# Filling the empty edge slots of a two-layer graph kernel with spread row numbers

## Chip, cores and metric

One NeuronCore of one Trainium2 chip. The metric is the device time of one execution in microseconds (us); a lower number is better. Three runs of the kernel before are at hand, and one further execution was recorded by the hardware profiler.

## What is computed

A graph of 6250 nodes (128 features, f32) and 206,250 directed edges (`src`, `dst`) goes through two attention layers.

```python
h = jnp.maximum(_layernorm(x), 0.0)
x = x + layer0(h)      # per edge: q of src, k and v of dst, 8 heads, clip, exp, sum over edges of src, normalise
h = jnp.maximum(_layernorm(x), 0.0)
x = x + layer1(h)      # per edge: cosine of h[src] and h[dst] times beta, softmax over edges of src, sum of h[dst]
```

In both layers every edge needs one row of a table in HBM by its `dst`, and the result is summed by its `src`.

## The kernel before, in words

**Sorting.** `sort_and_project` sorts the edges by the block of 128 nodes that `src` lies in (49 blocks). The edges stand as 128 partitions x 1620 columns and are taken in 18 chunks of 90 columns (NCHUNK, CHUNK). Edges of one chunk and block are laid into rows of 4 slots (ROW). One slot is an int32, `dst * 256 + (src & 127) + 1` (PACK is 256), and a slot with a low byte of 0 matches no node. Rows are written to the DRAM tensor `sorted_edges` by indirect DMAs of POOL (L389, 23 per chunk, 414 in all). A block's rows are padded to whole groups of 128 rows. A group is thus 128 partitions x 4 slots = 512 slots (GT is 4), and the arrays hold GROUPS = 456 groups, NT = 1824 slots per partition. Counted from the edge list, 439 groups hold edges; the last 17, groups 439 to 455, hold none. In the last group of each of the 49 blocks a part of the upper partitions is empty too: 4309 rows in all, some 88 of the 128 as a mean. The third kind of empty slot, inside rows that the sort does write (1282 slots), comes from the sort's own matmul and is 0.

**The fill.** Since only rows with edges are written, the slots of `sorted_edges` must hold something before the sort begins. DVE sets the SBUF tile `slots` to 0 (L596; it is part of the tile `slot_words`), SP waits for it and stores it to `sorted_edges` (L291, L292), then POOL waits until that store has landed (`s_filled`) and overwrites `slot_words` with `row_no`, an iota of 2944 elements (L381). ACT reads `row_no` at L532. On SP's queue the loads of the weights, gamma, beta and `cos_beta` stand behind the store (L294 to L297), and the stores of the counts (L301) behind those. POOL's queue holds the constants (L349 to L378) ahead of L381 and the 414 scatters after it. At the end of the sort, SP loads `slots` back (L342). DVE then splits them in place: the low byte less 1 goes to `loc`, and the upper bits, the row number to gather, stay in `slots`.

**The edge layers.** `layer0_edges` and `layer1_edges` walk over all 456 groups. For every group POOL issues four indirect DMAs, one for each slot column (L830 in `gather_groups`), each of which fetches 128 rows, one per partition: of `kv_table`, 1024 bytes a row, in layer 0, and of `h_table`, 520 bytes a row, in layer 1. The destinations are rings of 8 groups (`kv_rows`) and 12 groups (`h_rows`); before a group POOL waits for its row numbers (ACT, L934 and L1216) and for the ring slot's last reader: DVE's `vx` (L1013) in layer 0, PE's sums (L1294) in layer 1. DVE waits for the gathers of a group at L1005 (layer 0) and L1336 (layer 1), the first operations that read the gathered rows. PE multiplies by one-hot matrices made from `loc` (L968 and L982 in layer 0; L1264, L1277, L1286, L1294 in layer 1), and DVE adds up in SBUF (L1036, L1319). The last group of layer 0 must be added up before `between_layers` starts (L1099), and that of layer 1 before `finish` (L1380). An empty slot is gathered like any other; its one-hot row is zero, so what was fetched adds nothing.

Of the kernel before, what the change touches and what calls it, by code (L numbers as in the profile page):

```python
# [15 lines left out]
P = 128  # L16
N = 6250
# [34 lines left out]
ROOM = GROUPS + NCHUNK * CG  # L52
NT = GT * GROUPS
PACK = 256

RING0 = 8
NEAR = 4
# [47 lines left out]
def sort_and_project(nc, mem, dram, ins):  # L105

    src, dst, x, wq, wk, wv, gamma, beta, cos_beta = ins
    with ExitStack() as ctx:
# [3 lines left out]
        def sem(name):  # L112
            return ctx.enter_context(nc.semaphore(name))
# [3 lines left out]
        slots, loc_f, blkid, gb_sb, cb_sb = mem["slots"], mem["loc"], mem["blkid"], mem["gb"], mem["cb"]  # L117
# [77 lines left out]
        s_pool = sem("s_pool")  # L195
        s_pads = sem("s_pads")
        s_src, s_dst, s_x, s_w, s_gb = (sem(n) for n in ("s_src", "s_dst", "s_x", "s_w", "s_gb"))
        s_filled = sem("s_filled")
        s_v = sem("s_v")
        s_prep = sem("s_prep")  # L200
# [55 lines left out]
        def every_chunk(eng, chunk):  # L256

            turns = NCHUNK // 2
            for r in range(2 * PEEL):
                chunk(r // 2, r % 2)  # L260
            with eng.Fori(PEEL, turns - 1) as t:
                for r in range(2):
                    chunk(t, r)
            for r in range(2):
                chunk(turns - 1, r)
# [6 lines left out]
        def tiles_of(t, r, half):  # L272

            if isinstance(t, int) and not 1 <= t < NCHUNK // 2 - 1:
                return None
            s = 2 * r + half
            return 4 * t - 4 + s, (t - 1) * (4 * QT - 1) + QT * s, QT - s // 3

        def load_ends(eng, tile, edges, done):

            for a, b in ((0, 96), (96, 112), (112, P - 1)):
                if a == 96:
                    eng.wait_ge(s_pads, 2)
                eng.dma_start(tile[a:b, :], edges[a * COLS:b * COLS].rearrange("(p c) -> p c", c=COLS)).then_inc(done, 16)
            eng.dma_start(tile[P - 1:P, 0:LASTROW],
                          edges[(P - 1) * COLS:E].rearrange("(p c) -> p c", p=1)).then_inc(done, 16)

        @block.sync
        def _(sp):
            load_ends(sp, src_i, src, s_src)  # L290
            sp.wait_ge(s_pads, 4)  # L291
            sp.dma_start(slots_d, slots[:, :]).then_inc(s_filled, 16)  # L292
            for k, w in enumerate((wq, wk, wv)):
                sp.dma_start(w_sb[:, k * D:(k + 1) * D], w).then_inc(s_w, 16)  # L294
            for k, w in enumerate((gamma, beta)):
                sp.dma_start(gb_sb[:, k, :], w.rearrange("(o f) -> o f", o=1).broadcast_to((P, D))).then_inc(s_gb, 16)
            sp.dma_start(cb_sb[:, 0:1], cos_beta.rearrange("(o f) -> o f", o=1).broadcast_to((P, 1))).then_inc(s_gb, 16)  # L297

            for g in range(NCHUNK // CSTORE):
                sp.wait_ge(s_cntrow, CSTORE * (g + 1))  # L300
                sp.dma_start(dram["counts"][g * CSTORE:(g + 1) * CSTORE, :].rearrange("(o k) n -> o k n", o=1),  # L301
                             cnt_row[:, g % 2, :, :]).then_inc(s_cntd[g % 2], 16)
            for r in range(2):
                sp.wait_ge(s_cntd[r], 16 * (NCHUNK // CSTORE // 2))
            sp.dma_start(cnt[:, :].rearrange("b (k j) -> b k j", j=STEP),
                         dram["counts"].rearrange("k (b j) -> b k j", j=STEP)).then_inc(s_cntb, 16)

            sp.wait_ge(s_offc, 1)
            for part in range(2):
                sp.dma_start(dram["offs"][part].rearrange("k (b j) -> b k j", j=STEP),  # L310
                             off_parts[:, part, :].rearrange("b (k j) -> b k j", j=STEP)).then_inc(s_offd, 16)
            sp.wait_ge(s_offd, 32)
            for r in range(2):
                sp.dma_start(offrow[:, r:r + 1, :], dram["offs"][:, r:r + 1, :]).then_inc(s_row[r], 16)

            def stores(t, r):

                for half in range(2):
                    tiles = tiles_of(t, r, half)  # L320
                    if tiles:
                        s, first_tile, n = tiles
                        sp.wait_ge(s_hnow, s + 1)
                        sp.dma_start(h_sb[:, ds(first_tile, n), :], h_now[:, half, 0:n, :]).then_inc(s_hd[half], 16)
                for half in range(2):
                    tiles = tiles_of(t, r, half)
                    if tiles:
                        s, first_tile, n = tiles
                        sp.wait_ge(s_kv, s + 1)
                        sp.dma_start(dram["kv"].rearrange("(t p) f -> p t f", p=P)[:, ds(first_tile, n), :],  # L330
                                     kv[:, half, 0:n, :]).then_inc(s_kvd[half], 16)

            def loads(t, r):
                if not (isinstance(t, int) and t == NCHUNK // 2 - 1):
                    sp.wait_ge(s_rank, SPC * (2 * t + r) + 1)
                    sp.dma_start(offrow[:, r:r + 1, :], dram["offs"][:, ds(2 * t + r + 2, 1), :]).then_inc(s_row[r], 16)
                stores(t, r)
            every_chunk(sp, loads)
            sp.wait_ge(s_sorted, 1)
            sp.dma_start(slots[:, :], slots_d).then_inc(s_back, 16)  # L340
            for half in range(2):
                sp.wait_ge(s_kvd[half], 16 * (NCHUNK - 4))  # L342
                sp.wait_ge(s_hd[half], 16 * (NCHUNK - 4))
            sp.wait_ge(s_gb, 48)
            sp.wait_ge(s_filled, 16)

        @block.gpsimd
        def _(pool):
# [16 lines left out]
                                    base=0, pattern=[[1, P]], channel_multiplier=-1).then_inc(s_const, 1)  # L365
            nc.gpsimd.affine_select(out=ident[:, :], in_=ident[:, :], compare_op=ALU.not_equal, fill=1.0,
                                    base=0, pattern=[[-1, P]], channel_multiplier=1).then_inc(s_const, 1)
            nc.gpsimd.affine_select(out=keep[:, :], in_=keep[:, :], compare_op=ALU.not_equal, fill=0.0,
                                    base=-NBLK, pattern=[[0, 1]], channel_multiplier=1).then_inc(s_const, 1)
            nc.gpsimd.affine_select(out=room[:, :], in_=room[:, :], compare_op=ALU.is_equal, fill=0.0,  # L370
                                    base=-NBLK, pattern=[[0, NCHUNK]], channel_multiplier=1).then_inc(s_const, 1)
            nc.gpsimd.affine_select(out=bidiag[:, :], in_=bidiag[:, :], compare_op=ALU.not_equal, fill=1.0,
                                    base=0, pattern=[[-1, P]], channel_multiplier=1).then_inc(s_pool, 1)
            pool.wait_ge(s_pool, 6)
            nc.gpsimd.affine_select(out=bidiag[:, :], in_=bidiag[:, :], compare_op=ALU.not_equal, fill=-1.0,
                                    base=1, pattern=[[-1, P]], channel_multiplier=1).then_inc(s_pool, 1)
            pool.wait_ge(s_pool, 7)
            nc.gpsimd.affine_select(out=bidiag[:, :], in_=bidiag[:, :], compare_op=ALU.not_equal, fill=1.0,  # L378
                                    base=-NBLK, pattern=[[N, P]], channel_multiplier=1).then_inc(s_const, 1)
            pool.wait_ge(s_filled, 16)  # L380
            nc.gpsimd.iota(row_no, [[1, CG * P]], base=0, channel_multiplier=0,  # L381
                           allow_small_or_imprecise_dtypes=True).then_inc(s_const, 1)
# [209 lines left out]
        def _(dve):  # L592
            nc.vector.memset(src_i[96:P, LASTROW:COLS], PAD_SRC).then_inc(s_pads, 1)
            nc.vector.memset(dst_i[96:P, LASTROW:COLS], 0).then_inc(s_pads, 1)
            nc.vector.memset(x_sb[:, LASTB, :], 0.0).then_inc(s_pads, 1)
            nc.vector.memset(slots[:, :], 0).then_inc(s_pads, 1)  # L596
            nc.vector.memset(ones_b[:, :], 1.0).then_inc(s_prep, 1)
            nc.vector.memset(ones_2[:, :], 1.0).then_inc(s_prep, 1)
            tt, ts, stt = nc.vector.tensor_tensor, nc.vector.tensor_scalar, nc.vector.scalar_tensor_tensor
# [26 lines left out]
            link(ts(src_i[:, :], src_i[:, :], P - 1, None, ALU.bitwise_and))  # L626
            link(ts(pk_f[:, :], dst_i[:, :], float(PACK), 1.0, ALU.mult, ALU.add))
            tt(pk_f[:, :], pk_f[:, :], src_i[:, :], ALU.add).then_inc(s_packed, 1)
# [149 lines left out]
            for m in range(SPC):  # L778
# [10 lines left out]
            dve.wait_ge(s_back, 16)  # L789
            link(nc.vector.tensor_scalar(loc_f[:, :].bitcast(i32), slots[:, :], PACK - 1, None, ALU.bitwise_and))  # L790
            link(nc.vector.tensor_scalar(loc_f[:, :], loc_f[:, :].bitcast(i32), -1.0, None, ALU.add))
            link(nc.vector.tensor_scalar(slots[:, :], slots[:, :], PACK.bit_length() - 1, None,
                                         ALU.logical_shift_right))
# [656 lines left out]
```

## Time and profile before

| | us |
|---|---|
| median of 3 runs | 5818.73 |
| lowest and highest | 5814.07 and 5819.33 |
| the profiled execution | 5821.99 |
| its span, first to last instruction | 5820.3 |

| engine | busy us | share of the span |
|---|---|---|
| PE matmul | 4527.6 | 78% |
| POOL | 4147.2 | 71% |
| DVE | 4060.3 | 70% |
| ACT | 2159.7 | 37% |

The profiled execution's own time lies 1.7 us above its span and 3.3 us above the median of the runs. In the trace, the sort lasts until about 891, layer 0 gathers from 892 to 3250 and ends at 3288, layer 1 gathers from 3433 to 5754 and ends at 5797; the output is stored until 5820. "Busy" leaves out the issue of plain DMAs; POOL's indirect DMAs are counted as busy for the time in which POOL builds their descriptors, not for the transfer. Granted clock 1.00 in a stretch is TensorE's 2.4 GHz level, and 0.50 is 1.2 GHz.

### The profile page before, as it was taken

What the parts mean: (1) busy time and instruction counts of PE and PEld (TensorE: products, weight loads), DVE (VectorE), ACT (ScalarE), POOL (GpSimd) and SP (SyncE); (2) the same over time, 40 slices, a digit from 0 to 9 for tenths busy, and PEclk for the clock granted to TensorE, in tenths of its full rate; (3) what the DMA queues carried; (4) which work ended last, traced back from release to release, by engine and by line L of the source; (5) the groups of instructions that cost most, each with busy time, mean ns of one, the idle gap of its engine ahead of it and who ended that gap; (6) DMA issues with size and microseconds to landing.
All of it is one profiled execution on the core that took longest, in us unless ns stands there. A gap on an engine that the chain in (4) does not pass through costs nothing. (4 is left out here: it accounts for less than half of the span.)

```text
span 5820.3 us, 108286 instructions
## 1 busy us (share of the span) xinstructions
PE 4527.6 (78%) x25285; PEld 3846.5 (66%) x25286; DVE 4060.3 (70%) x11508; ACT 2159.7 (37%) x8114; POOL 4147.2 (71%) x4084
## 2 busy tenths in 40 slices
PE   5888866777777777777777338989888888888887
PEld 2777755666656666666655227878787778777776
DVE  8988956666766666666666676666666666666665
ACT  4988850000000000000000025555556555555554
POOL 0788877777777777777777237777777777777773
PEclk7888866666676666666666557777878888888886
DMA  1000003333333333333334422222222222222227
GB/s 43 15 18 18 18 5 98 101 101 101 101 102 102 102 102 102 102 102 102 101 102 96 42 44 55 54 53 54 54 51 54 54 54 53 54 53 54 53 53 50
DMA packets 192388, 388.47 MB, mean 67 GB/s; under 512 B 78472, under 2 KB 102546, under 8 KB 192150
## 3 DMA queue, kind: packets, MB, share of 16 engines
q0 software_dynamic: 159168, 361.59, 27.1%
q1 hardware_dynamic: 31146, 20.67, 1.4%
q10 hardware_dynamic: 1836, 4.03, 0.3%
q14 instruction: 209, 1.71, 0.1%
q8 instruction: 29, 0.48, 0.0%
HBM read 367.60 MB, written 15.20 MB: 66 GB/s over the span
## 5 line engine op out<-in xcount | busy, mean ns | idle before, releaser
L830 POOL DMA_INDIRECT h_rows<-h_table,idx_ring x1824 | 1745.4, 957 | 758.6 <-issue 533.7
L830 POOL DMA_INDIRECT kv_rows<-kv_table,idx_ring x1824 | 1803.6, 989 | 556.5 <-issue 555.3
L968 PE MATMUL psum<-q_sb,hotT 128*128 x3648 | 784.9, 383 | 435.5 <-DVE prod L1005 434.2
L968 PEld LDWEIGHTS psum<-q_sb,hotT 128*128 128x128 f32 x3648 | 678.7, 278 | 543.9 <-issue 543.4
L982 PE MATMUL psum<-vx,hot 128*128 128x136 f32 x3648 | 837.9, 399 | 151.6 <-DVE acc L1036 150.1
L947 ACT ACTIVATE vx<-clip 128x32 f32<-128x32 f32 x456 | 104.5, 229 | 2242.7 <-DVE clip L1029 2242.7
L982 PEld LDWEIGHTS psum<-vx,hot 128*128 128x128 f32 x3648 | 722.5, 286 | 317.5 <-issue 245.1
L389 POOL DMA_INDIRECT sorted_edges<-stage,addr x414 | 587.5, 1419 | 275.5 <-ACT stage L539 149.6
L1005 DVE TENSOR_TENSOR prod<-psum,kv_rows 128x512 f32<-128x512 f32 x456 | 315.3, 691 | 630.8 <-DMA kv_rows<-kv_table,idx_ring 630.1
L1336 DVE SCALAR_TENSOR_TENSOR prod<-psum,h_rows 128x128 f32<-128x128 f32 x1824 | 529.3, 346 | 240.3 <-DMA h_rows<-h_table,idx_ring 227.8
L1294 PE MATMUL psum<-h_rows,hotw 128*128 128x129 f32 x3648 | 652.0, 333 | 0.0
L1264 PE MATMUL psum<-q_sb,acc 128*128 x3648 | 620.3, 326 | 21.4 <-DVE prod L1336 20.7
L1264 PEld LDWEIGHTS psum<-q_sb,acc 128*128 128x128 f32 x3648 | 579.0, 241 | 29.8 <-issue 28.7
L1224 ACT ACTIVATE hotl<-hot,logit 128x128 f32<-128x128 bf16 x1824 | 589.5, 394 | 0.0
L1224 ACT ACTIVATE hotw<-hot,wgt 128x128 f32<-128x128 bf16 x1824 | 587.3, 393 | 0.2
L562 ACT ACTIVATE ends<-is_place,pk_now 128x92 f32<-128x92 bf16 x1440 | 517.3, 451 | 134.7 <-DVE is_place L748 134.5
L1294 PEld LDWEIGHTS psum<-h_rows,hotw 128*128 128x128 f32 x3648 | 565.6, 236 | 0.0
L1319 DVE SCALAR_TENSOR_TENSOR h_sb<-h_sb,corr,psum 128x129 f32 x456 | 159.1, 349 | 574.8 <-issue 379.8
L1277 PE MATMUL psum<-ident,hotl 128*128 128x128 f32 x1824 | 347.2, 321 | 268.4 <-DVE gmax L1329 267.4
L855 PE MATMUL psum<-rows,pick_row 4*128 4x512 bf16 x912 | 431.4, 473 | 154.6 <-DMA rows<-loc_rows 154.1
L1286 PEld LDWEIGHTS psum<-newtop,acc 128*128 128x128 f32 x3648 | 538.1, 226 | 0.3 <-issue 0.3
L1286 PE MATMUL psum<-newtop,acc 128*128 128x1 f32 x3648 | 517.4, 263 | 0.1
(206 smaller groups left out, 5994.5 us busy)
## 6 DMA issues: line engine op xcount, KB each, us to landing
kv_rows<-kv_table,idx_ring POOLq DMA_INDIRECT x1824
h_rows<-h_table,idx_ring POOLq DMA_INDIRECT x1824
sorted_edges<-stage,addr POOLq DMA_INDIRECT x414, 2.3
kv_table<-kv SPq DMA_DIRECT2D x21, 256.0 KB, 2.1
rows<-loc_rows SPq DMA_DIRECT2D x228, 4.0 KB
h_table<-acc SPq DMA_DIRECT2D x1, 3185.0 KB, 19.2
out<-q_sb SPq DMA_DIRECT2D x2, 1536.0 KB
h_sb<-h_now SPq DMA_DIRECT2D x21, 128.0 KB, 2.0
```

The source lines that it names most:

```text
L389: pool.indirect_dma_start(out=dram["sorted"], out_offset=bass.IndirectOffsetOnAxis(ap=addr[:, r, g:g + 1], axis=0), in_=stage[:, r, g * RO ...
L562: last = nc.scalar.activation(to_place[:, k, c, :], is_place[:, k, :, c], ACT.Copy, scale=pk_now[:, r, BATCH * b + c:BATCH * b + c + 1])
L830: pool.indirect_dma_start(out=G[:, u, j, :], out_offset=None, in_=table, in_offset=bass.IndirectOffsetOnAxis(ap=idx[:, u, j:j + 1], axis=0 ...
L855: nc.tensor.matmul(out, pick_row[:, g_u % FOUR, :], rows[:, h, :], start=True, stop=True).then_inc(s_spread, 1)
L968: last = nc.tensor.matmul(Q_ps[k][:, j * P:(j + 1) * P], hotT[:, k, j * P:(j + 1) * P], q_sb[:, ds(blk, 1), :].rearrange("p o f -> p (o f) ...
L982: last = nc.tensor.matmul(S_ps[(u - 3) % 2], hot[:, k, j * P:(j + 1) * P], vx[:, k, j, :], start=(j == 0), stop=(j == GT - 1))
L1224: last = nc.scalar.activation(out[:, j * P:(j + 1) * P], hot[:, u, :, j], ACT.Copy, scale=scale[:, j:j + 1])
L1264: last = nc.tensor.matmul(Q_ps[k][:, j * P:(j + 1) * P], hotT[:, (u + 1) % RING1, j * P:(j + 1) * P], q_sb[:, ds(blk, 1), :].rearrange("p ...
L1277: last = nc.tensor.transpose(L_ps[u % 2][:, j * P:(j + 1) * P], hotl[:, (u - 2) % TRIO, j * P:(j + 1) * P], ident[:, :])
L1286: last = nc.tensor.matmul(E_ps[u % 2][:, j:j + 1], hotT[:, n, j * P:(j + 1) * P], newtop[:, n:n + 1], start=True, stop=True)
L1294: last = nc.tensor.matmul(S_ps[u % 2], hotw[:, (u - 8) % TRIO, j * P:(j + 1) * P], G[:, (u - 8) % RING1, j, 0:AW1], start=(j == 0), stop=( ...
L1336: last = nc.vector.scalar_tensor_tensor(prod[:, j * P:(j + 1) * P], Q_ps[u % 2][:, j * P:(j + 1) * P], G[:, u, j, D + 1:TW], G[:, u, j, 0: ...
```

## The change

The zero fill by DVE goes. POOL writes the tile instead, by an iota after its constants: slot column j of partition p gets the value `256 * j + p * 34 * 256`. Its low byte is 0, so it matches no node, and its upper bits name row `j + 34 * p`. FILL_STEP is (6250 - 1824) // 127 = 34, and the highest row is 1823 + 34 * 127 = 6141. In one gather of 128 partitions the empty slots then name rows that stand 34 apart, 34,816 bytes in `kv_table` and 17,680 bytes in `h_table`. SP waits for POOL's `s_filler` in place of DVE's fourth `s_pads`.

```diff
+FILL_STEP = (N - NT) // (P - 1)
...
+        s_filler = sem("s_filler")
...
         def _(sp):
             load_ends(sp, src_i, src, s_src)
-            sp.wait_ge(s_pads, 4)
+            sp.wait_ge(s_filler, 1)
             sp.dma_start(slots_d, slots[:, :]).then_inc(s_filled, 16)
...
                                     base=-NBLK, pattern=[[N, P]], channel_multiplier=1).then_inc(s_const, 1)
+            nc.gpsimd.iota(slots[:, :], [[PACK, NT]], base=0, channel_multiplier=FILL_STEP * PACK).then_inc(s_filler, 1)
             pool.wait_ge(s_filled, 16)
...
             nc.vector.memset(x_sb[:, LASTB, :], 0.0).then_inc(s_pads, 1)
-            nc.vector.memset(slots[:, :], 0).then_inc(s_pads, 1)
```

## Rows read from the trace of the kernel before

**Rows 1.** The page: DMA share in 40 slices of the span, in tenths.
```profile
DMA  1000003333333333333334422222222222222227
```
**Rows 2.** The page, costliest groups: busy, mean ns of one, idle before, releaser.
```profile
L830 POOL DMA_INDIRECT h_rows<-h_table,idx_ring x1824 | 1745.4, 957 | 758.6 <-issue 533.7
L830 POOL DMA_INDIRECT kv_rows<-kv_table,idx_ring x1824 | 1803.6, 989 | 556.5 <-issue 555.3
```
**Rows 3.** Waits of POOL inside layer 0, 900 to 3160: total us, times, longest.
```profile
POOL kv_rows L830 <- issue: 532.4, 1747, 0.3
```
**Rows 4.** Windows: stretch, PE, PEld, DVE, ACT, POOL busy, clock, DMA share, GB/s.
```profile
2400.00:2900.00 500.00, 384.36 (x1642) 308.50 (x1643) 347.29 (x678) 30.38 (x194) 382.36 (x387) 0.66 0.36 102
...
3179.00:3250.00 71.00, 45.79 (x181) 36.30 (x182) 39.61 (x77) 3.19 (x19) 54.24 (x56) 0.60 0.90 78
4400.00:4900.00 500.00, 436.33 (x2878) 392.45 (x2878) 333.74 (x1580) 294.09 (x1188) 379.46 (x396) 0.83 0.24 54
5670.00:5760.00 90.00, 81.06 (x386) 72.80 (x387) 47.04 (x222) 40.70 (x159) 56.75 (x60) 0.59 0.95 41
```
**Rows 5.** Timeline of POOL, layer 0: start, us; fourth gathers of groups 438 and 455.
```profile
3161.84 0.95 POOL L830 DMA_INDIRECT kv_rows<-kv_table,idx_ring  x1 [0.30 <-issue]
...
3249.80 0.95 POOL L830 DMA_INDIRECT kv_rows<-kv_table,idx_ring  x1 [0.30 <-issue]
```
**Rows 6.** Timeline of DVE, layer 0: first use of groups 438, 439, 455; next stage.
```profile
3164.61 0.69 DVE L1005 TENSOR_TENSOR prod<-psum,kv_rows 128x512 f32<-128x512 f32 x1 [1.41 <-DMA kv_rows<-kv_table,idx_ring]
...
3172.14 0.69 DVE L1005 TENSOR_TENSOR prod<-psum,kv_rows 128x512 f32<-128x512 f32 x1 [3.75 <-DMA kv_rows<-kv_table,idx_ring]
...
3279.04 0.69 DVE L1005 TENSOR_TENSOR prod<-psum,kv_rows 128x512 f32<-128x512 f32 x1 [3.41 <-DMA kv_rows<-kv_table,idx_ring]
...
3287.80 0.56 DVE L1099 TENSOR_SCALAR rden<-acc 128x392 f32<-128x392 f32 x1 [0.33 <-PEq L860]
```
**Rows 7.** Timeline of POOL, layer 1: fourth gathers of groups 438, 447, 455.
```profile
5659.02 0.95 POOL L830 DMA_INDIRECT h_rows<-h_table,idx_ring  x1 [0.30 <-issue]
...
5704.08 0.95 POOL L830 DMA_INDIRECT h_rows<-h_table,idx_ring  x1 [0.30 <-issue]
...
5753.84 0.94 POOL L830 DMA_INDIRECT h_rows<-h_table,idx_ring  x1 [0.30 <-issue]
```
**Rows 8.** Timeline of DVE, layer 1: first use of groups 438, 455; next stage.
```profile
5661.62 0.35 DVE L1336 SCALAR_TENSOR_TENSOR prod<-psum,h_rows 128x128 f32<-128x128 f32 x1 [0.71 <-DMA h_rows<-h_table,idx_ring]
...
5774.84 0.35 DVE L1336 SCALAR_TENSOR_TENSOR prod<-psum,h_rows 128x128 f32<-128x128 f32 x1 [1.42 <-DMA h_rows<-h_table,idx_ring]
...
5797.29 0.47 DVE L1380 RECIPROCAL den<-h_sb 128x49 f32<-128x49 f32 x1 [0.33 <-PEq L1139]
```
**Rows 9.** Waits of POOL in layer 1, 3430 to 5797.
```profile
POOL h_rows L830 <- ACT idx_ring L1216: 184.9, 11, 181.9
```
**Rows 10.** Windows of 10 us in layer 1, columns as in rows 4.
```profile
4320.00:4330.00 10.00, 10.00 (x45) 9.34 (x46) 4.04 (x18) 5.37 (x21) 5.67 (x6) 0.50 0.20 47
...
5690.00:5700.00 10.00, 10.00 (x45) 9.33 (x45) 5.67 (x26) 5.93 (x24) 7.59 (x8) 0.50 0.93 41
```
**Rows 11.** Timeline of POOL at the start.
```profile
6.46 0.51 POOL L359 IOTA start<- 128x456 f32 x1
...
8.70 0.29 POOL L378 TENSOR_SCALAR_AFFINE_SELECT bidiag<-bidiag 128x128 f32<-128x128 f32 x1
14.72 2.58 POOL L381 IOTA slot_words<- 128x2944 f32 x1 [5.72 <-DMA sorted_edges<-slot_words]
```
**Rows 12.** Timeline of SP's queue at the start.
```profile
5.47 0.36 SPq L292 DMA_DIRECT2D sorted_edges<-slot_words  x1
...
26.71 48.26 SPq L301 DMA_DIRECT2D column_counts<-to_part  x6
```
**Rows 13.** Timeline of DVE at the start.
```profile
12.28 1.00 DVE L604 TENSOR_SCALAR pk_f<-ends 128x1620 int32<-128x1620 int32 x1 [6.70 <-DMA ends<-in_src]
```
**Rows 14.** Timeline of ACT: first read of `row_no`.
```profile
85.87 2.73 ACT L532 ACTIVATE start<-slot_words,edge 50x2944 bf16<-50x2944 f32 x1
```

## The prediction

> **What bounds the kernel now.** I read the page first, then the waits, then windows of 10 to 500 us, and last the timelines at the two ends of the edge layers.
>
> The row of DMA shares shows the sort, then layer 0 (tenths of 3), then layer 1 (tenths of 2). The last slice of each layer stands out: a 4 and a 7 [rows 1]. The costliest groups are POOL's gathers, 1824 in each layer. In layer 0 POOL is busy 1803.6 us and idle 556.5, together 2360.1 or 5.18 us for each of 456 groups [rows 2]. Its idle time consists of gaps of at most 0.3 us that nothing releases [rows 3], so in layer 0 POOL issues without pause and never waits for its ring. The layer cannot end before POOL's last issue, and as long as gathers land quickly it ends just behind it. In layer 1 POOL is busy 1745.4 and idle 758.6 [rows 2], 181.9 of it in one wait before the first group [rows 9]. Of the remaining 576.7, layer 0's plain gaps make 556.5, so 20.2 us are true stalls. Unstalled, a group costs (1745.4 + 556.5) / 456 = 5.05 us. Layer 1 is bound by POOL's issue as well, for nearly all of its length.
>
> The windows show what happens to the transfers [rows 4]. In mid-layer the 16 DMA engines are busy 0.36 of the time and move 102 GB/s (layer 0), 0.24 and 54 GB/s (layer 1). In the two tails, where only empty groups are left, they are busy 0.90 and 0.95 of the time and move only 78 and 41 GB/s. Full engines would move 102 / 0.36 = 283 and 54 / 0.24 = 225 GB/s of ordinary rows, but 87 and 43 GB/s in the tails: the same gather of the same size is 3.3 and 5.2 times as slow. The one thing special in these groups is that all 512 slots name row 0.
>
> The end of layer 0 says what that costs. Group 438, the last with edges, is used 3164.61 - 3161.84 = 2.77 us after its fourth gather was issued. Group 455 is used 3279.04 - 3249.80 = 29.24 us after its own [rows 5, 6]. Between groups 439 and 455 the uses stand (3279.04 - 3172.14) / 16 = 6.68 us apart, while POOL issues a group each (3249.80 - 3161.84) / 17 = 5.17 us. The transfers fall behind and DVE waits for them before each use.
>
> **The change, part by part.**
>
> *Layer 0, tail.* The empty groups now name 128 different rows per gather. If those move like ordinary rows, the use follows the issue by 2.77 us again: 29.24 - 2.77 = **26.5 us saved**. POOL's own pace stays as it is, since it was not stalled. The 8.8 us from the last use to the next stage (3287.80 - 3279.04 [rows 6]) stay. How much slower than ordinary rows may the new ones be? POOL offers 4 x 128 x 1024 bytes in 5.17 us, 101 GB/s, against 283: they may be 2.8 times as slow before anything shows. I take full saving; the bounds are 0 (as slow as row 0) and 26.5.
>
> Here a rule can be held against the row. The Trainium skill (DMA: Bandwidth & Descriptors, section Anatomy of one DMA) fits one DMA issued by POOL as 2.0 us plus its bytes over 436 GB/s, so 2.3 us for these 131,072 bytes and 2.15 us for a gather of layer 1. By that fit the two tails together would give back some 1.3 us more than by the rows; I keep the rows.
>
> *Layer 1, tail.* It has two terms. The delay from fourth gather to first use is 5661.62 - 5659.02 = 2.60 us for group 438 and 5774.84 - 5753.84 = 21.00 us for group 455 [rows 7, 8]. PE sometimes lags a little in this layer, so I take 3.0 for the ordinary delay: 18.0 us. And here POOL did stall: late gathers held back PE's sums, whose end frees a ring slot. The 8 groups from 447 to 455 took 5753.84 - 5704.08 = 49.8 us [rows 7]; at 5.05 each they take 40.4. That is 9.4 us more, and together **27.4 us saved**. The 22.4 us from the last first use to `finish` [rows 8] stay. The margin is larger than in layer 0: 266,240 bytes in 5.05 us are 53 GB/s against 225. Bounds: 0 and 27.8 (with the delay of 2.60).
>
> *Partly empty groups.* The last group of each block has some 88 rows of row 0 per gather. In layer 0 POOL never waits [rows 3], so nothing is won there. In layer 1, 20.2 - 9.4 = 10.8 us of stalls lie before the tail. Windows show that stretches of low TensorE clock can make such stalls: at a granted clock of 0.50 PE is busy 10.00 of 10 us and POOL gets through 6 gathers where it usually has 8, with a DMA share of only 0.20, so no slow gather [rows 10]. I take 0 here; bounds 0 and 10.8 saved.
>
> *The front.* DVE's fill goes; DVE then waits 6.70 us for `in_src` anyway [rows 13], worth nothing. POOL's iota over 1824 elements isn't in the trace. Between 456 elements in 0.51 us and 2944 in 2.58 us [rows 11] the slope is 0.83 ns an element, which gives 1.65 us; bounds 0.51 and 2.58. It starts at 8.70 + 0.29 = 8.99, ends near 10.7, and SP's store goes out 5.2 us later than at 5.47 [rows 12]. Behind it on SP's queue, the loads of weights, gamma, beta and `cos_beta` slip as much; the next entry, the first store of counts, is only due at 26.71 [rows 12], 16 us later, and six issues lie between (the store's own took 0.36 us). On POOL, L381 waits for the store. The store of 912 KB was issued at 5.47 and let L381 go at 14.72 [rows 11], 9.2 us; from 10.7 that gives 19.9, and the iota of `row_no` ends near 22.5. Its reader starts at 85.87 [rows 14]. So 63 us cover it. Without that cover the store's delay would cost 5.2 us, which is the upper bound; the lower is 0.5 us gained, should `in_src` land earlier. I take 0.
>
> *Sum.* 26.5 + 27.4 = 53.9 us. Against the profiled execution's own 5821.99 this gives 5768.1. The median of the runs is 3.3 lower, so the forecast is 5764.8, rounded to **5765 us**. By its bounds and the spread of the runs shown (5.3 us) this case covers 5757 to 5773.
>
> **The rivals.**
>
> *More is won.* The 10.8 us of stalls inside layer 1 could stem from the partly empty groups, one in nine, whose slow gathers let PE wait and its clock fall. Then the time is near 5754. Against it: 49 such groups and only half a tail's worth of stalls, and the low-clock window of rows 10 has no slow gather in it. Chance 0.10.
>
> *Layer 1 gives nothing back, since PE is the bound there.* In the old tail PE is busy 10.00 of 10 us at a clock of 0.50 with 45 matmuls [rows 10], just as in the mid-layer window where POOL made 6 gathers in 10 us, or 6.7 us a group. If PE stays low through the whole tail, 17 groups take 113 us from 5661.62, which ends at 5775: no gain over 5774.84. Only layer 0's 26.5 remain, 5792. Against it: over 4400 to 4900 the mean clock is 0.83, over the tail 0.59 [rows 4], so the fall goes with the late gathers. A low stretch of 50 us near the end would cost 7.5 groups x 1.6 = 12 us, 5777. Chance 0.06 for a loss beyond that.
>
> *Nothing changes, since row 0 isn't the cause.* If an empty group were slow whatever it names, the time stays at 5819. The ordinary rows of the same queue, size and destination speak against this. 
>
> *Slower.* The new rows stand 34 apart in every gather. If such a regular step falls on fewer parts of HBM than one row does, the tails get longer. The point is 6.68 us a group: beyond it by 0.34 us (5%), the 34 empty groups cost over 11.6 us. At twice the time of row 0 it would be 34 x 6.7 = 228 us, 6047. Nothing in the trace has this pattern; 128 different rows can hardly be worse than one. Chance 0.02.
>
> **How the numbers follow.** The forecast gets what is left, 0.79. The range of 5752 to 5780 holds it, the case with more won, and a low clock of 50 us near the end; some 0.1 lies outside. A difference of 0.2% (11.6 us) is about what a measurement of this kernel can tell from none. All cases but the last two are faster by more: 0.95 faster, 0.03 same, 0.02 slower.
>
> **What the changed profile would show.** DMA tenths of 3 and 2 up to each layer's end; in the tails DMA shares near 0.36 and 0.24; DVE's last L1005 some 3 us behind POOL's last gather, and L1336 likewise; POOL's idle time in layer 1 down by about 9 us. At the front, a POOL iota of 1.7 us and L381 near 20 us, with L532 still at 86. Wrong would be: full DMA engines in the tails (the rows collide), PE at 10.00 with clock 0.50 and POOL stalled at the end of layer 1 (PE binds), or a later L532.

## The result, and the profile after

The changed kernel takes 5811.49 us (median of 20 runs, 5798.51 to 5830.88), the kernel before 5824.65 us (20 runs, 5801.65 to 5844.35). The ratio is 0.998, with a 95% interval of 0.9971 to 0.9989. The change gains 13 us where 54 were forecast. The profiled execution has a span of 5798.8 us against 5820.3. Further down, one of the four executions of experiment e10 was a slow one, 6858.07 us at a granted clock of 1.00 where the three others show 0.74, and is left out of its numbers.

The page of the changed kernel, DMA shares in 40 slices, and the two groups of gathers (L832 is the old L830):

```profile
DMA  1000003333333333333333122222222222222222
...
L832 POOL DMA_INDIRECT h_rows<-h_table,idx_ring x1824 | 1767.6, 969 | 720.9 <-issue 523.8
L832 POOL DMA_INDIRECT kv_rows<-kv_table,idx_ring x1824 | 1818.4, 997 | 556.6 <-issue 555.0
```

Windows of the changed kernel, columns as in [rows 4]:

```profile
3179.00:3250.00 71.00, 55.31 (x232) 44.41 (x231) 47.46 (x95) 4.04 (x24) 54.39 (x55) 0.64 0.35 102
...
5670.00:5750.00 80.00, 70.19 (x450) 64.63 (x448) 52.37 (x251) 44.50 (x175) 61.38 (x62) 0.80 0.24 52
```

The busy DMA engines at the layers' ends are gone [rows 1, 4]. In the tails the shares are 0.35 and 0.24 at 102 and 52 GB/s, as in mid-layer. Timeline of the changed kernel, POOL's last gather and the first use of its group, layer 0 then layer 1 (5709.03 is the fourth gather of group 447):

```profile
3262.05 0.98 POOL L832 DMA_INDIRECT kv_rows<-kv_table,idx_ring  x1 [0.30 <-issue]
...
3264.88 0.69 DVE L1007 TENSOR_TENSOR prod<-psum,kv_rows 128x512 f32<-128x512 f32 x1 [2.20 <-DMA kv_rows<-kv_table,idx_ring]
3273.42 0.56 DVE L1101 TENSOR_SCALAR rden<-acc 128x392 f32<-128x392 f32 x1 [0.33 <-PEq L862]
...
5709.03 0.95 POOL L832 DMA_INDIRECT h_rows<-h_table,idx_ring  x1 [0.31 <-issue]
...
5750.59 0.95 POOL L832 DMA_INDIRECT h_rows<-h_table,idx_ring  x1 [0.30 <-issue]
...
5753.41 0.35 DVE L1338 SCALAR_TENSOR_TENSOR prod<-psum,h_rows 128x128 f32<-128x128 f32 x1 [1.00 <-DMA h_rows<-h_table,idx_ring]
```

The delay is 2.83 us in layer 0 (it was 29.24) and 2.82 us in layer 1 (21.00). So 26.4 and 18.2 us came back, where 26.5 and 18.0 were forecast. POOL's stalls at the end of layer 1 are gone too: the 8 groups from 447 to 455 take 5750.59 - 5709.03 = 41.6 us, and took 49.8 [rows 7]. What took most of it away again is in the middle: POOL's last gather of layer 0 is at 3262.05 instead of 3249.80 [rows 5], though the first one is 2.6 us earlier (889.0 instead of 891.6). All of POOL's gathers by their durations (minimum, median and maximum in ns), kernel before, then the changed one:

```profile
L830 POOL DMA_INDIRECT kv_rows<-kv_table,idx_ring x1824: 942/947/1445, 891.6 to 3249.8; - x183
L830 POOL DMA_INDIRECT h_rows<-h_table,idx_ring x1824: 939/945/1207, 3432.6 to 5753.8; - x183
```

```profile
L832 POOL DMA_INDIRECT kv_rows<-kv_table,idx_ring x1824: 949/954/1510, 889.0 to 3262.1; - x183
L832 POOL DMA_INDIRECT h_rows<-h_table,idx_ring x1824: 946/952/1217, 3416.8 to 5750.6; - x183
```

Minimum and median are both 7 ns higher, in both layers. POOL's busy time grows from 1803.6 to 1818.4 and from 1745.4 to 1767.6 us, 37.0 us in all. The account of the two spans: sort -2.6, first to last gather of layer 0 +14.8, delay -26.4, drain -0.2, from L1101 to layer 1's first gather -1.4, first to last gather of layer 1 +12.6, delay -18.2, the rest -0.1. That is -21.5, the whole difference. In layer 1, the 22.2 us of longer gathers are partly offset, because the stalls fall from 20.2 to 720.9 - 153.8 - 556.6 = 10.5 us; the 153.8 is POOL's wait for its first row numbers, the longest of the six in this line:

```profile
POOL h_rows L832 <- ACT idx_ring L1218: 155.3, 6, 153.8
```

The front of the changed kernel, POOL, SP's queue and DVE:

```profile
8.95 1.65 POOL L382 IOTA slot_words<- 128x1824 int32 x1
20.19 2.59 POOL L384 IOTA slot_words<- 128x2944 f32 x1 [9.59 <-DMA sorted_edges<-slot_words]
...
10.62 0.36 SPq L294 DMA_DIRECT2D sorted_edges<-slot_words  x1
...
13.30 1.00 DVE L606 TENSOR_SCALAR pk_f<-ends 128x1620 int32<-128x1620 int32 x1 [9.63 <-DMA ends<-in_src]
```

The iota took 1.65 us, SP's store left at 10.62, and `row_no` was ready near 22.8, long before its reader at 85.8. The front costs nothing, as forecast. (That layer 0 starts 2.6 us earlier isn't the change's doing: in e1, the kernel before once more, it starts at 889.3.) The front is also where the loss is set off, as the experiments show.

### The profile page after: what moved, and what is told of

The parts are those of the page before. It is cut to its first block and busy times, and to the rows that moved or that the text cites. A ratio compares the mean times of both kernels' runs of the same rounds, so it can differ in the third digit from the quotient of the medians.

```text
span 5798.8 us, 108286 instructions
## 1 busy us (share of the span) xinstructions
PE 4597.1 (79%) x25285; PEld 3902.6 (67%) x25286; DVE 4048.6 (70%) x11507; ACT 2159.4 (37%) x8114; POOL 4183.7 (72%) x4085
## 5 line engine op out<-in xcount | busy, mean ns | idle before, releaser
L832 POOL DMA_INDIRECT h_rows<-h_table,idx_ring x1824 | 1767.6, 969 | 720.9 <-issue 523.8
L832 POOL DMA_INDIRECT kv_rows<-kv_table,idx_ring x1824 | 1818.4, 997 | 556.6 <-issue 555.0
L970 PE MATMUL psum<-q_sb,hotT 128*128 x3648 | 801.4, 388 | 379.9 <-DVE prod L1007 379.2
L984 PE MATMUL psum<-vx,hot 128*128 128x136 f32 x3648 | 867.9, 410 | 139.9 <-DVE acc L1038 138.0
L984 PEld LDWEIGHTS psum<-vx,hot 128*128 128x128 f32 x3648 | 749.3, 295 | 307.2 <-issue 233.1
```

Source lines behind the costliest of these rows:

```text
L832: pool.indirect_dma_start(out=G[:, u, j, :], out_offset=None, in_=table, in_offset=bass.IndirectOffsetOnAxis(ap=idx[:, u, j:j + 1], axis=0 ...
L970: last = nc.tensor.matmul(Q_ps[k][:, j * P:(j + 1) * P], hotT[:, k, j * P:(j + 1) * P], q_sb[:, ds(blk, 1), :].rearrange("p o f -> p (o f) ...
L984: last = nc.tensor.matmul(S_ps[(u - 3) % 2], hot[:, k, j * P:(j + 1) * P], vx[:, k, j, :], start=(j == 0), stop=(j == GT - 1))
```

## The experiments

e1 to e4 ran on one chip, e5 to e8 on a second, e9 to e12 on a third, e13 to e16 on a fourth, e17 and e18 on a fifth, each time with the kernel before beside them. The ratio is to that one. "Gathers" is the median duration in layer 0, in ns, from the one profiled execution of each; the times are medians of 3 to 12 executions.

| run | POOL's added instruction | fill | gathers | median us | ratio (95% interval) |
|---|---|---|---|---|---|
| e1 | none | 0 | 946 | 5817.37 | 0.9998 (0.9987 to 1.0009) |
| e2 | int32 iota, full | spread | 954 | 5812.45 | 0.9984 (0.9975 to 0.9994) |
| e3 | int32 iota, full | 0 | 957 | 5853.97 | 1.0056 (1.0037 to 1.0076) |
| e4 | none | spread | 946 | 5773.90 | 0.9917 (0.9903 to 0.9930) |
| e5 | int32 memset, 1 element | spread | 949 | 6988.06 | 1.0006 (0.9996 to 1.0016) |
| e6 | int32 iota, 1 element | spread | 953 | 6984.31 | 0.9996 (0.9987 to 1.0006) |
| e7 | int32 iota, full; a memset less | spread | 957 | 6987.75 | 1.0000 (0.9990 to 1.0009) |
| e8 | int32 iota, full; 3 int32 memsets | spread | 957 | 6987.69 | 1.0003 (0.9993 to 1.0013) |
| e9 | as e2 | spread | 954 | 5805.82 | 0.9975 (0.9962 to 0.9988) |
| e10 | as e4 | spread | 946 | 5762.81 | 0.9899 (0.9874 to 0.9925) |
| e11 | as e3 | 0 | 954 | 5858.29 | 1.0066 (1.0046 to 1.0087) |
| e12 | as e2, as the first | spread | 954 | 5803.52 | 0.9975 (0.9963 to 0.9987) |
| e13 | f32 memset, 1 element | spread | 946 | 5770.16 | 0.9923 (0.9898 to 0.9948) |
| e14 | f32 iota, 1 element | spread | 949 | 5769.64 | 0.9917 (0.9896 to 0.9937) |
| e15 | int32 iota, 1 element | spread | 957 | 5808.49 | 0.9991 (0.9975 to 1.0008) |
| e16 | f32 iota, full, cast by DVE | spread | 946 | 5777.87 | 0.9934 (0.9910 to 0.9958) |
| e17 | int32 memset, 1 element | spread | 946 | 6971.37 | 0.9996 (0.9986 to 1.0005) |
| e18 | two int32 iotas, 1 element | spread | 953 | 6966.52 | 0.9987 (0.9978 to 0.9997) |

**Both kernels again, on one chip (e1, e2).** No edit.

> 

> The kernel before, once more, with a profile from the chip that the three others of this job run on. Theory T (row 0 is slow, the spread is not, and something else made POOL's gathers slower) and rival C (the slower issue is the chip's, not the change's) both expect ratio 1.000 and the two slow tails (last L1005 29 us behind the last gather). C expects POOL's gathers at the same median on this chip as in the changed kernel; T expects 0.947 us here and 0.953 us there.

> 

> The changed kernel, once more, on the same chip. T: POOL's gathers have a median of 0.953 us against 0.947 in the kernel before, together some 37 us more busy time over 3648 gathers, so the ratio is 0.997 to 0.998 though the tails give back 54 us. C (only another chip): POOL is as fast as in the kernel before on this chip, and the ratio is near 0.991.

The gathers of layer 0, e1 then e2:

```profile
L830 POOL DMA_INDIRECT kv_rows<-kv_table,idx_ring x1824: 942/946/1437, 889.3 to 3242.0; - x183
```

```profile
L832 POOL DMA_INDIRECT kv_rows<-kv_table,idx_ring x1824: 949/954/1413, 888.9 to 3262.6; - x183
```

On the same chip the 7 to 8 ns stay. The difference belongs to the kernel; the chip as its cause (C) is out.

**The iota without the spread (e3).**

```diff
-            nc.gpsimd.iota(slots[:, :], [[PACK, NT]], base=0, channel_multiplier=FILL_STEP * PACK).then_inc(s_filler, 1)
+            nc.gpsimd.iota(slots[:, :], [[0, NT]], base=0, channel_multiplier=0).then_inc(s_filler, 1)
```

> 

> The changed kernel with the iota's steps set to 0, so it writes zeros: POOL's added instruction and the new wait stay, the spread goes. Theory A (the added instruction in POOL's stream slows its later gathers): gathers at 0.953 us, tails slow as before, ratio 1.004 to 1.007. Theory B (the row numbers slow POOL's issue, by the traffic they make): gathers at 0.947 us and ratio 1.000. C: ratio 1.000.

```profile
L832 POOL DMA_INDIRECT kv_rows<-kv_table,idx_ring x1824: 952/957/1328, 889.1 to 3259.2; - x183
```

The gathers are slow though every empty slot names row 0, and the kernel is 33 us slower than before. In its tail the DMA engines are full again; window of e3, columns as in [rows 4]:

```profile
3180.00:3250.00 70.00, 43.61 (x171) 34.28 (x172) 37.07 (x72) 3.04 (x19) 53.56 (x55) 0.63 0.96 78
```

So the traffic of the spread rows does not slow the issue (B falls), and the slow tail comes from row 0.

**The spread without a POOL instruction (e4).** The zero fill stays. DVE adds the partition number to it (`rho`) and multiplies by 34 * 256, and SP waits for that.

```diff
-            sp.wait_ge(s_pads, 4)
+            sp.wait_ge(s_filler, 1)
...
+            dve.wait_ge(s_pads, 4)
+            dve.wait_ge(s_const, 4)
+            nc.vector.tensor_scalar(slots[:, :], slots[:, :], rho[:, 0:1], float(FILL_STEP * PACK), ALU.add,
+                                    ALU.mult).then_inc(s_filler, 1)
```

> 

> The kernel before, with POOL's instructions untouched; DVE adds the partition number times 34 * 256 to its zero fill (row 34p in every column). The 128 rows of a gather are all different. Theory A: gathers at 0.947 us, no slow tails, ratio 0.990 to 0.992 (54 us saved). Theory B: gathers at 0.953 us and ratio 0.997 to 0.998. If rows that repeat from gather to gather are slow too, the tails stay partly.

```profile
L836 POOL DMA_INDIRECT kv_rows<-kv_table,idx_ring x1824: 942/946/1356, 888.1 to 3245.7; - x183
L836 POOL DMA_INDIRECT h_rows<-h_table,idx_ring x1824: 938/944/1209, 3401.2 to 5716.9; - x183
```

Timeline of e4: the last gather of layer 0, its use, and the first use of the last group in layer 1:

```profile
3245.75 0.95 POOL L836 DMA_INDIRECT kv_rows<-kv_table,idx_ring  x1 [0.30 <-issue]
...
3248.51 0.69 DVE L1011 TENSOR_TENSOR prod<-psum,kv_rows 128x512 f32<-128x512 f32 x1 [2.14 <-DMA kv_rows<-kv_table,idx_ring]
...
5719.45 0.35 DVE L1342 SCALAR_TENSOR_TENSOR prod<-psum,h_rows 128x128 f32<-128x128 f32 x1 [0.74 <-DMA h_rows<-h_table,idx_ring]
```

Delays of 2.8 and 2.6 us and gathers of 946 ns together: 47 us faster than before, and 38.6 us faster than e2 beside it. POOL's busy time tells the same: 1803.4 + 1748.3 here, 1819.0 + 1767.0 in e2, 34.3 us. The 8 ns of median difference, over 3648 gathers, are 29 of these. It also shows that the same 128 rows may repeat from gather to gather without harm. Nothing between 128 different rows and one row for all was tried.

**Small instructions of two kinds, and a compensated count (e5 to e8).** e5 and e6 are e4 with one more POOL instruction where the changed kernel has its iota; e7 and e8 are edits of the changed kernel. `spare` is a new int32 tile of 8 columns that nothing reads.

```diff
e5: +            nc.gpsimd.memset(spare[:, 0:1], 0)
e6: +            nc.gpsimd.iota(spare[:, 0:1], [[0, 1]], base=0, channel_multiplier=1)
e7: -            nc.gpsimd.memset(keep[:, :], 1.0).then_inc(s_pool, 1)
e7: +            nc.vector.memset(keep[:, :], 1.0).then_inc(s_pool, 1)
e8: +            nc.gpsimd.memset(spare[:, 0:1], 0)      # and two more
```

> 

> The spread written by DVE (e4) plus one POOL memset of one element per partition where the changed kernel has its iota. Theory A1 (any instruction added ahead shifts POOL's later instructions, and their place in the stream sets the price): gathers at a median near 0.953 us instead of 0.946, ratio 0.996 to 0.999. Theory A2 (the int32 iota itself leaves POOL slower): gathers at 0.946 us, ratio 0.991 to 0.993.

> 

> The same with an int32 iota of one element per partition in place of the memset. A1: slow gathers (0.953 us) as in e5. A2: slow gathers here though not in e5. If neither is slow, it is the length of the iota, or the wait that hangs on it.

> 

> The changed kernel, and the memset of keep moved from POOL to DVE, so that POOL has as many instructions as before. A1: gathers back at 0.946 us, ratio 0.991 to 0.993 (54 us saved and none given back). A2: gathers stay at 0.953 us, ratio 0.997 to 0.999.

> 

> The changed kernel with three small POOL memsets more, so four instructions are added in all. A1 with a short period (four instructions of 64 bytes are one line of 256): gathers back at 0.946 us, ratio 0.991 to 0.993. A1 with another period: some other duration between 0.94 and 0.96. A2: 0.953 us.

The times of e5 to e8 tell nothing, since on this chip the kernel before itself took 6987.84 us. Waits of e5:

```profile
DVE hotT L1007 <- remote: 916.8, 114, 17.7
...
POOL kv_rows L838 <- DVE vx L1021: 643.5, 123, 12.5
```

POOL waits for DVE here, and layer 0 needs (3850.0 - 894.7) / 456 = 6.48 us a group, so neither 7 ns on a gather nor a transfer time of 6.68 us matters much. Why DVE stands still for up to 17.7 us was not tried. The durations of the gathers can still be read: 949 with the memset, 953 with the one-element iota, 957 in e7 and e8. Restoring POOL's count of instructions (e7) does not restore the gathers, and four instructions are no better than one (e8). So the place in the stream (A1) falls as the cause of the changed kernel's loss, and the kind is left. The levels are not quite those that A2 expected: 949 in e5 instead of 946, 957 in e7 instead of 953. The next runs had to say what a step of 3 ns means.

**Is the level the kernel's own? (e9 to e12).** Three repeats, and the changed kernel with its iota moved ahead of all of POOL's others.

```diff
+            nc.gpsimd.iota(slots[:, :], [[PACK, NT]], base=0, channel_multiplier=FILL_STEP * PACK).then_inc(s_filler, 1)
             nc.gpsimd.iota(bucket_no, [[1, NBUK], [0, CHUNK]], base=0, channel_multiplier=0,
...
-            nc.gpsimd.iota(slots[:, :], [[PACK, NT]], base=0, channel_multiplier=FILL_STEP * PACK).then_inc(s_filler, 1)
```

> 

> The changed kernel again, to see whether the level of POOL's gathers belongs to the kernel or to the load of a program. Theory K (it belongs to the kernel): the commonest duration is 0.953 us in layer 0 again. Theory R (it is drawn anew at each load): any of 0.946, 0.949, 0.953, 0.957. Where this chip binds the layers by POOL's issue, K expects ratio 0.997 to 0.999.

> 

> The spread written by DVE again. K: commonest gather 0.946 us and, where POOL binds, ratio 0.991 to 0.993. R: any level, and a ratio up to 1.001.

> 

> Zeros written by POOL's iota again. K: commonest gather 0.957 us, ratio near 1.0056 where POOL binds. R: any level.

> 

> The changed kernel with the iota as POOL's first instruction instead of after the constants; the later instructions stand in the same places of the stream as in the changed kernel, only those before move by one. If the place of the gather loops in the stream sets the level: 0.953 us as in the changed kernel. If what ran just before matters: another level. The store of the fill starts some 4 us earlier, which is hidden.

Neither K nor R is wholly right. The changed kernel is at 954 for the third time and e10 at 946 for the second, but the zero fill, at 957 in e3, is now at 954. Two later repeats show the same: e5 and e17 are one kernel at 949 and 946, e6 and e15 one kernel at 953 and 957. There are two families, 946 or 949 without an int32 iota and 953 or 957 with one (give or take 1); the step inside a family changes from run to run for the same kernel. Each repeat ran on another chip, so whether the step is drawn by the chip or at each start of the program stays open. Putting the iota first changes nothing (e12), so what ran just before the gathers does not matter either.

**The kind of instruction (e13 to e16).** e13 to e15 are e4 with one small POOL instruction each. e16 writes the changed kernel's fill as f32 and lets DVE turn it into int32; SP then waits for both.

```diff
e13: +            nc.gpsimd.memset(spare[:, 0:1], 0.0)
e14: +            nc.gpsimd.iota(spare[:, 0:1], [[0, 1]], base=0, channel_multiplier=1,
e14: +                           allow_small_or_imprecise_dtypes=True)
e15: +            nc.gpsimd.iota(spare[:, 0:1], [[0, 1]], base=0, channel_multiplier=1)
e16: +            nc.gpsimd.iota(slots[:, :].bitcast(f32), [[PACK, NT]], base=0, channel_multiplier=FILL_STEP * PACK,
e16: +                           allow_small_or_imprecise_dtypes=True).then_inc(s_filler, 1)
...
e16: +            dve.wait_ge(s_filler, 1)
e16: +            nc.vector.tensor_copy(slots[:, :], slots[:, :].bitcast(f32)).then_inc(s_filler, 1)
```

> 

> The spread by DVE (e4) plus one f32 memset of one element per partition on POOL, a kind that POOL's stream already has. Theory N (any added POOL instruction makes the later gathers slower): commonest gather in layer 0 above 0.946 us. Theory I (only an int32 iota does): 0.946 us. Where POOL binds, I expects ratio 0.990 to 0.992.

> 

> The same with an f32 iota of one element, again a kind that the stream already has. N: above 0.946 us. I: 0.946 us and ratio 0.990 to 0.992.

> 

> The same with an int32 iota of one element, as in e6, on another chip. I: 0.953 us, and where POOL binds a ratio of 0.996 to 0.999, since 3648 gathers at 7 ns and the longer ones that come with them cost 30 to 37 us. N: the same level as e13 and e14.

> 

> The changed kernel's fill, written by POOL as an f32 iota of the full size and turned into int32 by DVE, which is idle then. I: 0.946 us, no slow tails, ratio 0.990 to 0.992: the whole gain with the fill still on POOL. N: 0.949 to 0.957 us, ratio 0.995 to 1.000.

Gathers of layer 0 in e14, e15 and e16:

```profile
L839 POOL DMA_INDIRECT kv_rows<-kv_table,idx_ring x1824: 945/949/1421, 886.6 to 3246.9; - x183
```

```profile
L838 POOL DMA_INDIRECT kv_rows<-kv_table,idx_ring x1824: 952/957/1328, 892.8 to 3270.6; - x183
```

```profile
L835 POOL DMA_INDIRECT kv_rows<-kv_table,idx_ring x1824: 942/946/1277, 886.5 to 3243.6; - x183
```

`spare` is f32 in e14 and int32 in e15; otherwise they differ in nothing but the flag that the type needs. One int32 iota of one element costs 5808.49 - 5769.64 = 39 us. A full-size f32 iota costs nothing to be seen (e16). Theory I holds in all but the 949 of e14, where it expected 946: that is the step inside the family, and e14's time is that of e13. N falls, since e13 and e16 are at 946.

**Any int32 instruction, and twice (e17, e18).**

```diff
e17: +            nc.gpsimd.memset(spare[:, 0:1], 0)
e18: +            nc.gpsimd.iota(spare[:, 0:1], [[0, 1]], base=0, channel_multiplier=1)
e18: +            nc.gpsimd.iota(spare[:, 1:2], [[0, 1]], base=0, channel_multiplier=1)
```

> 

> The spread by DVE plus one int32 memset of one element on POOL, as in e5, on another chip. If only the int32 iota matters: commonest gather in layer 0 0.946 or 0.949 us and, where POOL binds, ratio 0.990 to 0.993. If any int32 instruction does: 0.953 or 0.957 us and 0.997 to 0.999.

> 

> The spread by DVE plus two int32 iotas of one element. If each such iota adds its 7 ns to all later gathers: 0.960 to 0.964 us, and a ratio near 1.004. If the first one changes a state once and for all: 0.953 or 0.957 us, ratio 0.997 to 1.000.

```profile
L838 POOL DMA_INDIRECT kv_rows<-kv_table,idx_ring x1824: 942/946/1404, 897.9 to 3841.2; - x183
```

```profile
L839 POOL DMA_INDIRECT kv_rows<-kv_table,idx_ring x1824: 949/953/1377, 894.9 to 3839.8; - x183
```

This chip too had the kernel before at 6975.98 us, so only the durations count. An int32 memset leaves the gathers at 946, and a second int32 iota adds nothing to the first. This fits a state that one int32 iota brings about and that lasts to the end of the program. The indirect DMAs of the sort, which stand behind the iota too, agree in their shortest one; kernel before, then the changed one:

```profile
L389 POOL DMA_INDIRECT sorted_edges<-stage,addr x414: 954/1144/3571, 166.9 to 879.3; - x138
```

```profile
L392 POOL DMA_INDIRECT sorted_edges<-stage,addr x414: 963/1143/3582, 166.5 to 876.8; - x138
```

But in every run here all indirect DMAs come after the iota. No run has it between two of them, so that it must be executed first, and not only be part of the program, is not shown.

## Why the prediction was wrong

- **What bounds the kernel: right.** POOL's issue bounds both layers. That is why 7 ns on an instruction of 0.95 us are seen in the total at all.
- **Tails: right.** Forecast delays of 2.77 and 3.0 us, measured 2.83 and 2.82, counted from the start of the issuing instruction, so 26.4 and 18.2 us came back. The Trainium skill's fit (DMA: Bandwidth & Descriptors, section Anatomy of one DMA), 2.3 and 2.15 us, was too short for both. Ordinary speed of the spread rows was right as well: DMA shares of 0.35 and 0.24.
- **Stalls of layer 1: right.** 9.4 us were to go from the tail; 9.7 went. The 10.8 us inside the layer are still there as 10.5 us, so the rival in which partly empty groups cause them is not borne out by this trace.
- **The front: the cost at the front was right, the term that mattered was absent.** The prediction priced the new iota as 1.65 us, bounds 0.51 and 2.58, and measured it is 1.65. The step that failed is "POOL's own pace stays as it is, since it was not stalled", with the bounds 0 and 26.5 set by the transfers alone. The pace changed: 3648 gathers became 7 to 8 ns longer, 34 to 38 us by POOL's busy time (e4 and e1 against e2). e3 shows it without the spread. No row of the kernel before could show it, but an operation without a row was taken as harmless beyond its own length, and the bounds had no room for an after-effect on the engine that binds.
- **The sum without that term: right within the noise.** e4, which has the change's effect and no int32 iota, takes 5773.90 us, 47 us below the kernel before beside it, and its repeat e10 5762.81 us, 57 us below; e13 and e14 gain 45 and 46. Forecast were 5765 and 53.9. The interval of e4's ratio, 0.9903 to 0.9930, is 41 to 56 us. The 5757 to 5773 given beside the sum does not follow from the bounds of its terms, which reach down to nothing saved; it was a guess at the spread.
- **Rivals.** None was this one. The nearest, "slower", looked for the loss in the transfers. PE did not bind the end of layer 1 either: in the tail it is busy 70.19 of 80 us at a granted clock of 0.80, and POOL does not stall. e3 shows the loss by itself: 33 us, and 38 in e11.

Why an int32 iota makes later gathers longer stays open. What the runs bound: among the instructions tried it takes int32 and iota together (e13, e14, e16, e17), not a certain size (e15), place (e12) or number (e18), and it touches the gathers of both layers alike. The Trainium skill (Advanced Engine Details and Errata, section Sequencer Memory) gives the cores of POOL an instruction cache of 16 KB in lines of 256 bytes; that other code in it leads to other durations would be in line with this, but no run here shows it.

## What to carry to other kernels

Padding indices should not all name one row: an indirect gather of 128 times the same row moved 78 and 41 GB/s here, where different rows move 102 and 54 at a third or a quarter of the engines' time, and the pile at the end of a stage is fully exposed. On an engine whose issue binds a long loop, price an added instruction by what the loop does after it as well as by its own length, and compare the median of the loop's instruction before and after. The fastest version is the spread written by DVE (e4, e10: ratios 0.9917 and 0.9899), 47 and 57 us faster than before; an f32 iota on POOL with a cast by DVE (e16, 0.9934) cannot be told from it.

## What the runs showed of the hardware that was not expected

- With one int32 iota on POOL, even of one element, at the start of the program, the median of the 128-row gathers behind it is 953 to 957 ns instead of 946 to 949, up to the last gather, 5.7 ms later in the changed kernel.
- For the same kernel these durations come in two levels some 3 ns apart (957 in e3, 954 in e11). Over 3648 gathers that would be 11 us, but the times do not show it: e3 has the ratio 1.0056, e11 with the shorter gathers 1.0066.
- On two of the five chips every execution of the kernel before took near 6988 or 6976 us instead of 5821. There POOL waits for DVE (643.5 us in e5), and none of these edits moves the time by more than 0.13%.
